# Order of the Wo sums on GpSimd, and the last feed-forward steps, in a fused gated cross-attention kernel

## What is computed

```python
xn = layernorm(x)
q = xn @ Wq                          # 32 heads of 128
k, v = concat([ctx, xn]) @ Wk, Wv    # 8 kv heads, 461 rows
q, k = rms_norm(q) * wq, rms_norm(k) * wk
probs = softmax(q @ k.T / sqrt(128))
x = x + tanh(g_xattn) * (probs @ v) @ Wo
y = layernorm(x)
top2 = top_k(softmax(y @ router_w.T + router_b), 2)
w = top2 gates, normalised, at the two experts
x = x + tanh(g_ffn) * sum_e (y @ A_e.T * w_e) @ B_e.T * 0.5
```

## Time and profile before

| | us |
|---|---|
| median of 3 runs | 1715.18 (1713.99 to 1717.83) |
| the profiled execution | 1715.65 |
| its span | 1713.8 |
| PE busy | 1665.8 |
| DVE busy | 1239.6 |
| POOL busy | 873.9 |
| ACT busy | 865.1 |

### The profile page before, as it was taken

How to read it: one execution, slowest core, us unless ns; L and a number is a source line. 1 busy time by engine, 2 the same in 40 slices (tenths; PEclk the granted TensorE clock), 3 DMA queues, 4 the chain that set the end, 5 groups by cost and what they waited for, 6 DMA issues and landing times.

```text
span 1713.8 us, 26112 instructions
## 1 busy us (share of the span) xinstructions
PE 1665.8 (97%) x9120; PEld 1475.3 (86%) x9120; DVE 1239.6 (72%) x2078; ACT 865.1 (50%) x1647; POOL 873.9 (51%) x668
## 2 busy tenths in 40 slices
PE   7999999999999999999999999999999999999996
PEld 6788888678888869899999999999999889999994
DVE  7788776677777742777777777777776876557767
ACT  5445554454444432555666565665555666443321
POOL 1454444134443320766767667788786445543320
PEclk9999999999999999999999999999999999999998
DMA  5667778636666564456555554666756557676632
GB/s 196 161 181 233 235 210 241 183 108 186 162 184 154 140 239 150 138 159 191 188 156 187 182 179 160 213 217 216 232 181 215 170 205 267 212 275 229 241 116 68
DMA packets 238502, 323.86 MB, mean 189 GB/s; under 512 B 53300, under 2 KB 193396, under 8 KB 233380
## 3 DMA queue, kind: packets, MB, share of 16 engines
q1 hardware_dynamic: 237796, 315.65, 59.8%
q10 hardware_dynamic: 576, 6.55, 0.9%
HBM read 212.18 MB, written 109.97 MB: 188 GB/s over the span
## 4 chain that ended last, share of the span: by engine, by line
PE 70%; DVE 18%; issue 4%; ACT 4%; DMA 2%; POOL 0%; DVEq 0%; SPq 0%; ACTq 0%; POOLq 0%
PE bank L973 21%; PE bank L975 20%; PE bank L974 20%; DVE mx L1923 4%; PE bank L1111 3%; DVE wq_lo L1805 3%; DVE q_lo L1897 3%; PE bank L1078 2%; DVE pT_lo L1917 2%; DMA kT_d<-kst 1%; PE bank L1007 1%; ACT pr L1539 1%; DVE q_raw L1875 1%; DVE nm L1929 1%; DVE wo_lo L1943 1%
## 5 line engine op out<-in xcount | busy, mean ns | idle before, releaser
L901 POOL TENSOR_SCALAR pr<-pr,rr 100x461 f32<-100x461 f32 x256 | 370.2, 1454 | 231.6 <-DVE rr L1938 231.6
L973 PE MATMUL bank<-w_hi,a_hi 128*128 128x512 f32 (+1 forms) x856 | 340.8, 398 | 11.7 <-DVE a_lo L1713 8.6
L975 PE MATMUL bank<-w_hi,a_lo 128*128 128x512 f32 (+1 forms) x856 | 334.8, 391 | 0.0
L974 PE MATMUL bank<-w_lo,a_hi 128*128 128x512 f32 (+1 forms) x856 | 334.3, 390 | 0.0
L1539 ACT ACTIVATE pr<-bank,nm,rq 100x461 f32<-100x461 f32 x256 | 188.8, 737 | 187.6 <-DVE nm L1929 186.2
L855 POOL TENSOR_TENSOR msk<-ssk,epst 128x4 f32<-128x4 f32 (+1 forms) x60 | 23.5, 391 | 348.5 <-DVE ssk L1744 348.5
L973 PEld LDWEIGHTS bank<-w_hi,a_hi 128*128 128x128 f32 (+1 forms) x856 | 157.8, 184 | 48.8 <-issue 9.7
L1923 DVE TENSOR_REDUCE mx<-bank 100x1 f32<-100x461 f32 x256 | 160.6, 627 | 48.7 <-PE bank L975 47.2
L975 PEld LDWEIGHTS bank<-w_hi,a_lo 128*128 128x128 f32 (+1 forms) x856 | 157.5, 184 | 38.0
L973 PE MATMUL bank<-xT_hi,wq_hi 128*128 128x400 f32 x512 | 188.9, 369 | 0.5 <-issue 0.5
L974 PEld LDWEIGHTS bank<-w_lo,a_hi 128*128 128x128 f32 (+1 forms) x856 | 158.0, 185 | 34.8
(11 more groups left out here) (154 smaller groups left out, 3635.1 us busy)
## 6 DMA issues: line engine op xcount, KB each, us to landing
kT_d<-kst SPq DMA_DIRECT2D x56, 512.0 KB, 5.7
v_d<-vst SPq DMA_DIRECT2D x56, 512.0 KB
kT<-kT_d SPq DMA_DIRECT2D x64, 361.0 KB, 4.5
kvr<-ctxT SPq DMA_DIRECT2D x44, 512.0 KB, 6.2
wq_raw<-Wq SPq DMA_DIRECT2D x32, 512.0 KB, 5.8
tb<-Wo SPq DMA_DIRECT2D x16, 1024.0 KB, 8.3
wt_d<-tb SPq DMA_DIRECT2D x16, 1024.0 KB, 8.0
wo_raw<-wt_d SPq DMA_DIRECT2D x16, 1024.0 KB, 7.4
```

Source lines behind the costliest of these rows:

```text
L901: pool.tensor_scalar(pr[0:NQ, u % 2, i], pr[0:NQ, u % 2, i], rr[0:NQ, i:i + 1], None, ALU.mult).then_inc(p_done, 1)
L973: pe.matmul(o, lh, rh, start=start, stop=False, skip_group_check=more)
L974: pe.matmul(o, lh, rl, start=False, stop=False, skip_group_check=more)
L975: return pe.matmul(o, ll, rh, start=False, stop=stop, skip_group_check=more)
```

## The change

On POOL, the first four steps' 16 weight sums come before `unit_rms(0)`; the other 48 come one to a unit (0 to 47), ahead of the unit's scales and behind a wait for `nm` of its first head. The differences are spread over units 8 to 52, behind the scales in every fourth unit up to 44 and in 48 and 52, ahead of them in 48 to 51. `unit_rms` moves behind the scales two units earlier. On SP, the first two blocks of Wo are loaded before the next heads of Wq, steps 0 to 3 are stored and steps 2 to 5 loaded ahead of unit 0's loads, and from then on a step's successor is loaded right behind its store. At the end, `low_rank(3)` goes ahead of the last head of the last half chunk, `route_top(3)` ahead of `accumulators(P3)`, and `norm` of elements 4 to 7 goes to ACT, as scale and bias of one activation; POOL makes the bias with two more small operations. The lists of the last four elements are set anew on PE, ACT and DVE.

```diff
@@ -148,13 +148,20 @@
 WT_OF = {P6: 0, P4: 1, P7: 2, P5: 3}
 WT_OPS = ((2, 3, 2, True), (0, 2, 0, False), (3, 3, 0, True), (1, 1, 0, True))
 WT_STEPS = GQ * R
-WT_AT = {}
-for _n in range(4 * WT_STEPS):
-    WT_AT.setdefault(max(-1, (_n - 4) * 6 // 7), []).append(_n)
-WT_DONE = {n: next(u for u in WT_AT if 4 * n + 3 in WT_AT[u]) for n in range(WT_STEPS)}
-
-S3_AT = 34
+
+WT_FIRST = 4
+WT_DONE = [4 * (n - WT_FIRST) + 3 for n in range(WT_STEPS)]
+WT_LAST = WT_DONE[-1]
+
+
 S3_STEPS = GQ * TB
+S3_TIMES = sorted([(u, 1) for u in range(B, WT_LAST + 6, TB)] + [(WT_LAST + 1 + n, 0) for n in range(4)])[:S3_STEPS]
+S3_AT = {t: n for n, t in enumerate(S3_TIMES)}
+S3_LOAD = {}
+S3_STORE = {}
+for _n, (_u, _i) in enumerate(S3_TIMES):
+    S3_LOAD.setdefault(_u - 1, []).append(_n)
+    S3_STORE.setdefault(_u + 1, []).append(_n)
 
 UPPER = (P5, P4)
 TAIL0 = FIRST_OF[P2]
@@ -733,23 +742,26 @@
 
             for n in range(AHEAD):
                 load_heads(n)
-                if n == AHEAD - 2:
+                if n == 0:
                     load_t(0)
                     load_t(1)
+                if n in (5, 6, 7, 8):
+                    store_t(n - 5)
+                    load_t(n - 3)
             for u in range(UNITS):
                 load_heads(u + AHEAD)
                 if 1 <= u < UNITS - 1:
                     load_kT(u + 1)
 
-                for n in range(WT_STEPS):
+                for n in range(WT_FIRST, WT_STEPS):
                     if u == WT_DONE[n] + 1:
                         store_t(n)
-                    if u == WT_DONE[n] + 2 and n + 2 < WT_STEPS:
-                        load_t(n + 2)
-                if 0 <= u - S3_AT - 2 < S3_STEPS:
-                    store_s3(u - S3_AT - 2)
-                if 0 <= u - S3_AT < S3_STEPS:
-                    load_s3(u - S3_AT)
+                        if n + 2 < WT_STEPS:
+                            load_t(n + 2)
+                for n in S3_STORE.get(u, ()):
+                    store_s3(n)
+                for n in S3_LOAD.get(u, ()):
+                    load_s3(n)
                 if u in (OUT0 - 2, OUT0 - 1):
                     load_chunk(u - OUT0 + 2)
                 if OUT0 + 1 <= u:
@@ -928,18 +940,23 @@
                 for b in range(TB):
                     pool.tensor_tensor(to[:, b], x[:, b], y[:, b], ALU.add if o == P5 else ALU.subtract).then_inc(at_sum, 1)
 
+            for i in range(4 * WT_FIRST):
+                weight_sum(i)
             unit_rms(0)
-            for i in WT_AT[-1]:
-                weight_sum(i)
             for u in range(UNITS):
-                if u % TB == TB - 1 and u + 1 < UNITS:
-                    unit_rms(u + 1)
+
+                if u <= WT_LAST:
+                    pool.wait_ge(nm_done, 4 * u + 1)
+                    weight_sum(4 * WT_FIRST + u)
+                if (u, 0) in S3_AT:
+                    pool.wait_ge(nm_done, 4 * u + 1)
+                    early_sum(S3_AT[u, 0])
                 for i in range(R):
                     scale(u, i)
-                for i in WT_AT.get(u, ()):
-                    weight_sum(i)
-                if 0 <= u - S3_AT - 1 < S3_STEPS:
-                    early_sum(u - S3_AT - 1)
+                if (u, 1) in S3_AT:
+                    early_sum(S3_AT[u, 1])
+                if u % TB == TB - 2 and u + 2 < UNITS:
+                    unit_rms(u + 2)
                 if u == UNITS - 2:
                     chunk_sums(FIRST_OF[P5])
             for m in range(FIRST_OF[P6], LAST_OF[P6] + 1):
@@ -966,6 +983,11 @@
                 pool.tensor_scalar(mv2[0:NQ, t, 0:1], mv[0:NQ, t, 1:2], 1.0, LN_EPS, ALU.mult, ALU.add).then_inc(va2_done, 1)
                 pool.wait_ge(va2_done, t + 1)
                 pool.tensor_tensor(mv2[0:NQ, t, 1:2], mv2[0:NQ, t, 0:1], mhalf[0:NQ, 0:1], ALU.pow).then_inc(rs2_done, 1)
+                if t >= TB:
+                    pool.tensor_scalar(mv2[0:NQ, t, 2:3], mv[0:NQ, t, 0:1], -1.0, 0.0, ALU.mult, ALU.add).then_inc(mean_done, 1)
+                    pool.wait_ge(mean_done, t - TB + 1)
+                    pool.wait_ge(rs2_done, t + 1)
+                    pool.tensor_tensor(mv2[0:NQ, t, 3:4], mv2[0:NQ, t, 2:3], mv2[0:NQ, t, 1:2], ALU.mult).then_inc(scaled_done, 1)
 
         @block.tensor
         def _(pe):
@@ -1307,14 +1329,16 @@
             for n in range(4 * GQ):
                 for i in range(2):
                     chunk_head(TAIL0 + n // 2, n % 2 * 2 + i)
+                    if (n, i) == (4 * GQ - 1, 0):
+                        low_rank(TB - 1)
                 for i, t in sorted(FFN_AT.get(n, ())):
-                    stages[i](t)
+                    if n < 4 * GQ - 1:
+                        stages[i](t)
 
             a, b, c, d = range(TB, B)
-            for do, t in ((turn_out, a), (turn_out, b), (turn_h, a - 1), (turn_out, c), (turn_y, a), (up, a - 1), (low_rank, a),
-                          (turn_out, d),
-                          (turn_y, b), (low_rank, b), (turn_h, a), (turn_y, c), (up, a), (low_rank, c), (turn_h, b), (up, b),
-                          (turn_y, d), (low_rank, d), (turn_h, c), (up, c), (turn_h, d), (up, d)):
+            for do, t in ((turn_out, a), (turn_out, b), (turn_h, a - 1), (up, a - 1), (turn_out, c), (turn_y, a), (low_rank, a),
+                          (turn_out, d), (turn_y, b), (low_rank, b), (turn_h, a), (turn_y, c), (up, a), (low_rank, c),
+                          (turn_h, b), (up, b), (turn_y, d), (low_rank, d), (turn_h, c), (up, c), (turn_h, d), (up, d)):
                 do(t)
 
         @block.scalar
@@ -1656,6 +1680,13 @@
                 if t == 2:
                     chunk_heads(G)
 
+            def norm(t):
+
+                act.wait_ge(scaled_done, t - TB + 1)
+                act.wait_ge(t2_done, t - 1)
+                act.activation(y[0:NQ, t % 2], x1[0:NQ, t % 4], ACT.Identity, bias=mv2[0:NQ, t, 3:4],
+                               scale=mv2[0:NQ, t, 1:2]).then_inc(y_done, 1)
+
             def turned_y(t):
                 act.wait_ge(t2_done, t + 1)
                 if t >= 2:
@@ -1696,11 +1727,10 @@
                         turned_h(t)
                 if m < len(CHUNKS):
                     (chunk_heads if n % 2 else chunk_weights)(m)
-            exps2(TB - 1)
-            turned_h(TB - 1)
             a, b, c, d = range(TB, B)
-            for do, t in ((turned_y, a), (exps2, a), (turned_y, b), (turned_h, a), (turned_y, c), (exps2, b),
-                          (turned_h, b), (turned_y, d), (exps2, c), (turned_h, c), (exps2, d), (turned_h, d)):
+            for do, t in ((exps2, a - 1), (turned_h, a - 1), (norm, a), (turned_y, a), (norm, b), (exps2, a), (turned_y, b),
+                          (norm, c), (turned_h, a), (turned_y, c), (exps2, b), (norm, d), (turned_h, b), (exps2, c),
+                          (turned_y, d), (turned_h, c), (exps2, d), (turned_h, d)):
                 do(t)
 
         @block.vector
@@ -2154,13 +2184,11 @@
                 for i, t in at_last:
                     if i == 0:
                         residual(t)
+            route_top(TB - 1)
             accumulators(P3)
-
             a, b, c, d = range(TB, B)
-            for do, t in ((route_top, a - 1), (residual, a), (route_gates, a - 1), (norm, a), (residual, b), (final, a - 1),
-                          (residual, c), (norm, b), (route, a),
-                          (norm, c), (residual, d), (route, b), (final, a), (norm, d), (route, c), (final, b), (route, d),
-                          (final, c), (final, d)):
+            for do, t in ((route_gates, a - 1), (residual, a), (residual, b), (final, a - 1), (residual, c), (route, a),
+                          (residual, d), (route, b), (final, a), (route, c), (final, b), (route, d), (final, c), (final, d)):
                 do(t)
 
 
```

More of the change, by code:

```diff
@@ L199, in build @@
         mv = sb("mv", [P, B, 2])
-        mv2 = sb("mv2", [P, B, 2])
+        mv2 = sb("mv2", [P, B, 4])
         rstd = sb("rstd", [P, B, 2])
@@ L412, in build @@
         va2_done = sem("va2_done")
+        mean_done = sem("mean_done")
+        scaled_done = sem("scaled_done")
         rs2_done = sem("rs2_done")
```

## The result

The changed kernel took 1728.51 us in the median of four runs (1723.72 to 1732.78), the kernel before 1715.73 on the same chip: ratio 1.0073, 95% interval 1.0044 to 1.0102. Run again later beside other kernels it took 1725.92 (five runs) against 1716.02, ratio 1.0054 (1.0040 to 1.0068). It is slower by 10 to 13 us, outside my range (1710.5 to 1722.0). The profiled execution was the fastest of its four: 1723.72, span 1721.9, which is 8.1 us over the span of before.

What follows compares the result with a forecast made beforehand. PE, busy 97% of the span, was taken as the bound, so time follows PE's waits. Start +17, slots -14 and end -2.5 sum to +0.5 against the profiled 1715.65, on the median 1715.7 us; range 1710.5 to 1722.

Steps and rivals of the forecast that it cites:

- part 2: Slots 2 to 54: weight sums moved away from DVE's `wq_lo` shorten the slots, -14 us, ends -12 and -14.8.
- the 0.8 that I left for other meetings: Slots: 0.8 us of the 14.8 held back for remaining meetings of POOL's work with DVE.
- Part 1: Start: sums ahead of `rq` wait for Wo loads and stores, PE idles; +17 us, ends 14 and 21.
- of an idle queue already: Start: argument against shorter transfers, claiming the earlier trace's load and store times already came from an idle queue.
- my two chains: Start: loads, stores and sums put `rq` at 704.4; SP's late Wq head puts `ms` at about 701.
- Part 3: End: four norms off DVE and two steps moved earlier; 3.2 + 0.8 less 1, counted as -2.5 us.
- Slower: Start: dearer hole, PE waiting again in slot 0, half clock through slot 1; start +21, total +7, 1722; chance 0.22.
- The slots do not get what the change says: Slots: scale meets `q_lo`, or sum or `unit_rms` meets `wq_lo` or `nm`; half of 14.8 stays, +7, 1722; chance 0.10.
- Faster: Start chain shorter (links 1.3 us less), slot 1 at full clock, end gives 4.5; -6.5, 1709; chance 0.18.
- the signs: Expected: PE idle 682 to about 701, `rq` 703 to 706, slot 1 near 714, slots 2 to 55 near 603.
- two signs of being wrong: Start and slots: prediction wrong if `rq` comes before 698 or even slots stay above 11.6 us.

Runs made afterwards that it cites:

- wait_kept: Changed kernel with the next Wo block loaded one unit after the store, SP's wait for the store staying in the store's unit; 1719.52 us, ratio 1.0018.
- start_only: Kernel before with only the change's start (16 sums ahead of `unit_rms(0)`), other 48 sums behind the scales, one a unit; 1734.92 us, ratio 1.0108.
- wq_first: Changed kernel with Wo loads one unit after the store and the three Wq heads ahead of SP's starting stores and loads; 1721.93 us, ratio 1.0031.
- after_again: The changed kernel run a second time, nothing edited, beside the other kernels; 1725.92 us (1723.12 to 1726.97).
- two_soon: two_first with each Wo block loaded right behind its predecessor's store again; 1710.94 us, ratio 0.9966.
- tail_only: Kernel before with only the change's tail: norms on ACT, `low_rank(3)` and `route_top(3)` earlier, new lists; 1713.65 us, ratio 0.9982.
- load_later: Changed kernel with each next 1 MB Wo block loaded one unit after the store instead of right behind it; 1719.67 us, ratio 1.0020.
- two_first: Changed kernel with only 8 sums ahead of `rq`, 56 spread over units, differences behind scales, Wo loads one unit later; 1698.26 us, ratio 0.9888.
- sums_behind: load_later with the 48 slot sums put behind the four scales, without the wait for `nm`; 1732.69 us, ratio 1.0093.

## Why the prediction was wrong

Forecast +0.5, profile +8.1. The difference of 7.6 is 2.9 at the start, 5.4 in the slots and -0.8 at the end. By the prediction's own steps:

- **The step that failed** is in part 2: "SP now waits in every fourth slot for a store of 7 to 9 us; what stands behind it, `store_attn` and `load_vv`, waits for the slot's end anyway." The store's time was right (9.0) and so was the harmlessness of the wait (wait_kept). What I left out is what the wait releases: a load of 1 MB that enters the queue just ahead of the slot's `store_attn`, v and `kT`. `kT` then lands 8.0 us after its issue instead of 4.0, and the next slot's first scores need it. It cost 6.2 us in the slots (608.40 against 602.25), 5.2 in the second profile, and 6.5 in time (+9.9 against +3.4, each beside its own runs of before).
- **The rest of part 2** was right: `wq_lo` 1.23, even slots 11.3 to 11.4, and without the collision 602.25, which is the full 14.7 us; the 0.8 that I left for other meetings was not needed.
- **Part 1**, +17, was under-sized by 2.9 us (start_only: +18.7 in time): the first `nm` came 24.5 us late (710.74 against 686.20) and not 20.8, and slots 0 and 1 gave back some 4.6 and not 3.8. The mechanism held in each link, `ms` as releaser and half clock included. The term most off is the load of the fourth block, 5.8 us by the earlier trace rows and 9.1 measured, with a Wq head and a store issued behind it; the last four sums took 0.8 more than counted. The store's 4.5 instead of 5.7 gave back 1.2, and the load behind it, 6.9 instead of 5.8, took that again. That the rows were "of an idle queue already" was wrong for the store, which had two loads of `kT` behind it. The Trainium skill ("DMA: Bandwidth & Descriptors", "Anatomy of one DMA") gives an estimate of 4.4 us for 1 MB. The trace agrees for the store that was alone in the queue (4.5); the load of 5.8 in the earlier trace rows, with nothing issued behind it for 13 us, is over it, and so are the three others here, 6.9 to 9.1, which had company in the queue. Of my two chains the one of the sums is enough by itself (wq_first); whether the other would be was not tried.
- **Part 3**, -2.5, measured -3.3, -2.8 in time alone. But I counted 3.2 for the norms and 0.8 less 1 for the moved steps; the norms with the new lists give all of it, and `low_rank(3)` is 1.9 us long, not 1.
- **The rivals.** *Slower* named the right place and a start of +20, but for a reason that did not occur: PE waited again only briefly in slot 0 and was at full clock in slot 1. No rival had the collision. *The slots do not get what the change says* had the right half of the result by the wrong mechanism: no sum or scale meets `wq_lo`. *Faster* needed links 1.3 us shorter; one was.
- Of the signs, PE's idle time with `ms` as releaser (to 704.2, not 701), `wq_lo` and even slots came, and `rq` just missed its 703 to 706 (706.27); slots near 603 did not, and slot 1 near 714 came at 718.28. Neither of the two signs of being wrong appeared: they looked at `rq` and at even slots, and the loss was in odd ones.

What stays open: on the first chip the profiled run was 4.8 us under the median, on the second at the median, and only profiled runs show where time went. The remainder of the 12.8 us of the first comparison over the profile's 8.1 is not placed. The second profile of the same kernel, after_again, is 10.3 us over the span of before: +21.4 at the start (0.7 of it ahead of the changed part), -9.5 in the slots and -1.5 from slot 63 on. Why the collision is twice as dear in two_soon as in the changed kernel was not tried apart; its stores leave in other units.

## What to carry to other kernels

When a transfer is moved up, ask what lets it go and what is issued within the next microsecond: a large load released in mid-slot by the store before it can delay the small transfers that the next slot needs, though the wait itself costs nothing. Here one unit's delay of a load, whose data is needed much later, is worth 6 to 13 us. Work moved into idle time ahead of a critical small operation is free only as far as its data is already there: two blocks in two buffers cost nothing, the third and fourth, which need store and load in turn, cost about 20 us. The parts of such a change add (start_only +18.7, tail_only -2.8, and the slots' 14.7 less the 2.2 that start_only has already: +3.4, which is what load_later measured), so each can be judged, and kept, alone; two_first is what is left when the start's loss is taken out.

## What was not expected of the hardware

- A transfer's time went with what was issued behind it as well as ahead of it: a store of 1 MB took 4.5 us with nothing behind it and 5.7 with two loads of `kT` behind it; a load of 1 MB took 5.8 with nothing behind it, 6.9 with another megabyte 1.6 us behind, and 9.1 with half a megabyte 0.4 and 1 MB 2.2 us behind. No run varies only this. Behind a 1 MB load, 200 KB landed after 8.7 us (1.9 without it) and 361 KB after 8.0 (4.0).
- After 22 us without a matmul, PE was at 0.50 of its clock for 5.6 us (704.2 to 709.8) and then at full speed; the much shorter wait of before (2.79 us) was followed by a slot 1 of 14.1 us, and in two_first one of 0.76 us by a slot of 11.4 (granted clock 1.00).
- `q_lo`, too, is longer with the sums behind the scales: mean 1.52 us in sums_behind against 1.01 in load_later, for 50 of them. Between the kernel before and the changed one `q_lo` fell from 91.4 to 60.8 us over the whole run and `wq_lo` from 66.2 to 39.5; with the norms' 3.2 that is more than the 54.8 us by which DVE's busy time fell, in which overlapping instructions count once.
